# A state-space layer and a mixture of experts on one core: the state's output matmuls contract over 64 rows, in pairs

## What is computed

```
xz = layernorm(x) @ w_in                  # 256 -> 2 * 512, halves xp and z
xc = silu(causal 4-tap conv(xp) + conv_b) # per channel
h[t] = 0.9 * h[t-1] + 0.1 * (xc[t] @ w_B) # the state: 16 numbers per token
y = (h @ w_C) * silu(z)                   # 16 -> 512, gated
x = x + y @ w_out                         # 512 -> 256
n = layernorm(x)
e1, e2 = top 2 of 8 experts by (n[:, 0] @ Wr + br)        # per sequence
x = x + mean over e1, e2 of gelu(n @ W1[e] + b1[e]) @ W2[e] + b2[e]
```

## Time and profile before

| | |
|---|---|
| median of 3 runs | 507.81 us |
| the profiled execution | 506.41 us, of it span 504.6 us |
| PE | busy 499.1 us (99%), 3026 matmuls, granted clock full throughout |
| DVE / ACT / POOL | busy 451.8 (90%) / 400.6 (79%) / 348.7 us (69%) |
| state_out (L1490) | 64 matmuls of 128x512, mean 0.39 us each, 0.23 us from start to start |
| weight loads | 0.19 us each, normally beside the matmul before |

### The profile page before, as it was taken

The page is one execution under the profiler, slowest core; times in us unless marked ns, Lnnn a source line. Parts: engine busy times, 40 slices in busy tenths (PEclk is TensorE's granted clock), DMA queues, the critical chain, the costliest instruction groups (busy, mean ns, idle before and its releaser), DMA issues.

```text
span 504.6 us, 9913 instructions
## 1 busy us (share of the span) xinstructions
PE 499.1 (99%) x3026; PEld 438.7 (87%) x3026; DVE 451.8 (90%) x896; ACT 400.6 (79%) x692; POOL 348.7 (69%) x390
## 2 busy tenths in 40 slices
PE   7999999999999999999999999999999999999997
PEld 7888799888888888888888888888888888888997
DVE  6999899889998899989999899998999989996773
ACT  4986958878869789697887969879797888969454
POOL 4959587659593796928969197782977649773391
PEclk9999999999999999999999999999999999999999
DMA  8940105435251442606235170432604334130102
GB/s 258 292 185 7 37 1 168 125 127 168 73 183 40 162 129 83 208 15 196 81 125 166 42 224 25 166 125 86 205 36 138 117 125 126 52 116 1 42 2 84
DMA packets 53379, 57.28 MB, mean 114 GB/s; under 512 B 8682, under 2 KB 49642, under 8 KB 53226
## 3 DMA queue, kind: packets, MB, share of 16 engines
q1 hardware_dynamic: 51498, 56.67, 34.3%
q10 hardware_dynamic: 1856, 0.31, 0.3%
HBM read 35.46 MB, written 21.50 MB: 113 GB/s over the span
## 4 chain that ended last, share of the span: by engine, by line
PE 97%; DVE 1%; DMA 1%; issue 0%; DVEq 0%
PE blk L1294 16%; PE blk L1295 16%; PE blk L1301 16%; PE tok L1415 12%; PE tok L1417 11%; PE tok L1416 11%; PE turn L1466 3%; PE turn L1469 3%; PE blk L1490 3%; PE turn L1242 1%; PE tok L1294 1%; PE tok L1301 1%; PE tok L1295 1%; DMA x_mid<-in_L_attn_x 1%; DVE stats_t L917 0%; DVE normed L934 0%
## 5 line engine op out<-in xcount | busy, mean ns | idle before, releaser
L992 DVE SCALAR_TENSOR_TENSOR conv<-blk,tap_w,conv 128x512 f32<-128x512 f32 x192 | 130.1, 741 | 7.1 <-ACT conv L683 6.0
L488 POOL TENSOR_TENSOR y_lo<-gate,y_hi 128x512 fp32r<-128x512 f32 x57 | 72.2, 1299 | 35.1 <-ACT y_hi L611 35.1
L1294 PE MATMUL blk<-xn_hi,w_in_hi 128*128 128x512 f32 x228 | 89.4, 392 | 0.0
L1295 PE MATMUL blk<-xn_hi,w_in_lo 128*128 128x512 f32 x228 | 89.0, 391 | 0.0
L453 POOL TENSOR_TENSOR xc_lo<-conv,xc_hi 128x512 fp32r<-128x512 f32 x60 | 73.4, 1242 | 7.5 <-ACT xc_hi L611 7.3
L1415 PE MATMUL tok<-w_out_hi,y_hi 128*128 128x256 f32 x256 | 72.2, 282 | 0.0
L1417 PE MATMUL tok<-w_out_hi,y_lo 128*128 128x256 f32 x256 | 70.8, 277 | 0.0
L1416 PE MATMUL tok<-w_out_lo,y_hi 128*128 128x256 f32 x256 | 70.8, 276 | 0.0
L1301 PE MATMUL blk<-xn_lo,w_in_hi 128*128 128x512 f32 x228 | 70.3, 389 | 0.0
L1415 PE MATMUL tok<-w_hi,hid_hi 128*128 128x256 f32 x248 | 70.3, 283 | 0.0
L683 ACT ACTIVATE conv<-blk,tap_b,tap_w 128x512 f32<-128x512 f32 x64 | 49.1, 778 | 25.1 <-PE blk L1301 22.0
(11 more groups left out here) (189 smaller groups left out, 1318.2 us busy)
## 6 DMA issues: line engine op xcount, KB each, us to landing
spill<-normed SPq DMA_DIRECT2D x25, 512.0 KB, 2.8
normed<-spill SPq DMA_DIRECT2D x100, 128.0 KB, 2.8
out<-x_mid SPq DMA_DIRECT2D x30, 256.0 KB, 2.2
x_mid<-in_L_attn_x SPq DMA_DIRECT2D x29, 256.0 KB, 2.7
x_in<-in_L_attn_x SPq DMA_DIRECT2D x14, 512.0 KB, 4.4
w_all<-in_L_ffn_W SPq DMA_DIRECT2D x2, 2048.0 KB, 11.3
b_all<-in_L_ffn_b SPq DMA_DIRECT2D x1, 1024.0 KB, 13.4
gate<-in_L_attn_w_in SPq DMA_DIRECT2D x2, 256.0 KB, 4.8
```

The lines of the kernel that those rows point to most:

```text
L488: nc.gpsimd.tensor_tensor(y_lo[:, j, :], gate_of(o, j), y_hi[:, j, :].bitcast(F32), ALU.subtract).then_inc(y_lo_set, 1)
L992: nc.vector.scalar_tensor_tensor(cols, blk[j][:], tap_w[:, j, t:t + 1], cols, ALU.mult, ALU.add).then_inc(tap_added, 1)
L1294: mm(dst, whi(k), his(k), start=(k == 0), stop=False)
L1295: ins = mm(dst, wlo(k), his(k), start=False, stop=False)
```

## The change

Weights and state get another layout on the 128 rows: each half of 64 rows (rows 0 to 63, rows 64 to 127) now holds all the products, in four groups of 16, so that 64 rows are enough for one output block. Even blocks j contract over the lower half, odd blocks over the upper.

```
-                    mm(c_bank(a, j)[:], c_mix[:, j * P:(j + 1) * P], state_mix[:], start=True,
+                together = 2 if has_ffn(s) else 1
+                for i, j in enumerate(js):
+                    if i % together == 0:
+                        c_free(a, s, js[i + together - 1])
+                    rows = slice(j % 2 * HALF, (j % 2 + 1) * HALF)
+                    mm(c_bank(a, j)[:], c_mix[rows, j * P:(j + 1) * P], state_mix[rows, :], start=True,
```

```
# ACT state_hi
-                hi(state_mix[:], state[:, q, :]).then_inc(h_hi, 1)
+                hi(state_mix[:], state[:, q, :], sign_rows[STATE][:]).then_inc(h_hi, 1)
# DVE state_lo
-                lo(state_mix[P // 2:P, :], state[P // 2:P, q, :], state_mix[P // 2:P, :]).then_inc(h_lo, 1)
+                nc.vector.scalar_tensor_tensor(state_mix[:], state[:, q, :], low_rows[STATE][:], state_mix[:].bitcast(F32), ALU.mult,
+                                               ALU.add).then_inc(h_lo, 1)
# POOL state_lo, for chunk 1 alone
-                nc.gpsimd.tensor_tensor(state_mix[P // 2:P, :], state[P // 2:P, q, :],
-                                        state_mix[P // 2:P, :].bitcast(F32), ALU.subtract).then_inc(h_lo, 1)
+                nc.gpsimd.tensor_scalar(state[:, q, :], state[:, q, :], low_rows[STATE][:], None, ALU.mult).then_inc(h_masked, 1)
+                pool.wait_ge(h_masked, 1)
+                nc.gpsimd.tensor_tensor(state_mix[:], state[:, q, :], state_mix[:].bitcast(F32), ALU.add).then_inc(h_lo, 1)
# DVE, ahead of everything
+            def row_masks():
+                dve.wait_ge(consts_set, 3)
+                groups = ident[:].rearrange("p (h g i) -> p g h i", h=2, i=NST)
+                for i, group in enumerate(LOW_GROUP):
+                    nc.vector.tensor_reduce(low_rows[i][:], groups[:, group], axis=mybir.AxisListType.XY,
+                                            op=ALU.add).then_inc(rows_set, 1)
+                ...
```

More of the change, by code:

```diff
@@ L36, in build_block @@
     HALO = TAPS - 1
-    REP = P // (2 * NST)
-    assert PER == 2 and TT == 4 and KD == 2 and JD == 4 and JF == 4 and NST == 16 and E == 8
+    HALF = P // 2
+    STATE, WEIGHT = 0, 1
+    LOW_GROUP, REST_GROUP = (1, 2), 3
+    assert PER == 2 and TT == 4 and KD == 2 and JD == 4 and JF == 4 and HALF == 4 * NST and E == 8
     x_t = x.rearrange("b s d -> (b s) d").rearrange("(c n p) d -> c p n d", p=P, n=TT)
@@ L67, in build_block @@
         unused = sb("unused", [1, 1])
+        low_rows, sign_rows = [sb(f"low_rows{i}", [P, 1]) for i in range(2)], [sb(f"sign_rows{i}", [P, 1]) for i in range(2)]
         first_tok = sb("first_tok", [P, KD])
@@ L118, in build_block @@
         consts_set = sem("consts_set")
+        rows_set = sem("rows_set")
         w_hi_set = sem("w_hi_set")
@@ L149, in build_block @@
         u_ready, scanned = sem("u_ready"), sem("scanned")
-        h_hi, h_lo = sem("h_hi"), sem("h_lo")
+        h_hi, h_masked, h_lo = sem("h_hi"), sem("h_masked"), sem("h_lo")
         c_ready = sem("c_ready")
@@ L281, in has_ffn, with mix_cols @@
             return not isinstance(s, int) or s >= 2
+        def mix_cols(h, group):
+            return slice(h * HALF + group * NST, h * HALF + (group + 1) * NST)
         def half_rows(h):
@@ L515, in opening @@
                 norm1(1)
[L516 to L526, removed]
+                pool.wait_ge(w_hi_set, 5 + REST_GROUP)
+                for h in range(2):
+                    nc.gpsimd.tensor_tensor(b_mix[:, :, mix_cols(h, REST_GROUP)], wb_raw[:],
+                                            b_mix[:, :, mix_cols(h, 0)].bitcast(F32), ALU.subtract).then_inc(mix_lo_set, 1)
+                pool.wait_ge(rows_set, 4)
+                nc.gpsimd.tensor_scalar(state[:, 0, :], state[:, 0, :], low_rows[WEIGHT][:], None, ALU.mult).then_inc(mix_lo_set, 1)
+                pool.wait_ge(mix_lo_set, 3)
+                nc.gpsimd.tensor_tensor(c_mix[:], state[:, 0, :], c_mix[:].bitcast(F32), ALU.add).then_inc(mix_lo_set, 1)
+                pool.wait_ge(mix_lo_set, 4)
                 split_conv(0, (0, 1))
@@ L529, in opening @@
                 norm1(2)
-                pool.wait_ge(w_hi_set, 6 + REP)
+                pool.wait_ge(w_hi_set, 6 + REST_GROUP)
                 weights_lo(w_out_lo[:], raw_out, w_out_hi[:])
@@ L627, in mix_hi @@
                 hi(state[:, 0, :], raw_c, GAIN).then_inc(w_hi_set, 1)
[L628 to L631, removed]
+                for group in range(REST_GROUP):
+                    both = b_mix[:].rearrange("p j (h c) -> p j h c", h=2)[:, :, :, mix_cols(0, group)]
+                    hi(both, wb_raw[:].rearrange("p j (o s) -> p j o s", o=1).broadcast_to([P, JD, 2, NST])).then_inc(w_hi_set, 1)
+                act.wait_ge(w_hi_set, 4 + REST_GROUP)
+                act.wait_ge(rows_set, 4)
+                hi(c_mix[:], state[:, 0, :], sign_rows[WEIGHT][:]).then_inc(w_hi_set, 1)
             def turn1_hi(c):
@@ L1074, in route @@
                 nc.vector.max_index(expert[:], best[:], scores[:]).then_inc(route_step, 1)
+            def row_masks():
[4 more added lines that the diff above has]
+                                            op=ALU.add).then_inc(rows_set, 1)
+                for i in range(2):
+                    dve.wait_ge(rows_set, 1 + i)
+                    nc.vector.tensor_scalar(sign_rows[i][:], low_rows[i][:], -2.0, 1.0, ALU.mult, ALU.add).then_inc(rows_set, 1)
             def opening():
+                row_masks()
                 stats1_first(0)
@@ L1102, in opening @@
                 dve.wait_ge(consts_set, 4)
-                dve.wait_ge(mix_lo_set, REP + 2)
+                dve.wait_ge(mix_lo_set, 4)
                 scan(0, 0)
@@ L1472, in state_in, with c_free @@
                 ins.then_inc(u_ready, 1)
+            def c_free(a, s, j):
+                if has_ffn(s):
+                    pe.wait_ge(gelu_set, (s - 2) * JF + j + 1)
+                elif a == 0:
+                    pe.wait_ge(gate_set, JD + j + 1)
+                elif j == 0:
+                    pe.wait_ge(route_step, 1)
+                elif j == 1:
+                    pe.wait_ge(tap_added, last_tap(2, 2))
+                elif j == 2:
+                    pe.wait_ge(gate_set, 3 * JD - 1)
+                else:
+                    pe.wait_ge(tap_added, last_tap(2, 3))
             def state_out(a, s, js=range(JD)):
                 pe.wait_ge(h_lo, a + 1)
[L1476 to L1489, removed]
-                    mm(c_bank(a, j)[:], c_mix[:, j * P:(j + 1) * P], state_mix[:], start=True,
+                together = 2 if has_ffn(s) else 1
[4 more added lines that the diff above has]
+                    mm(c_bank(a, j)[:], c_mix[rows, j * P:(j + 1) * P], state_mix[rows, :], start=True,
                        stop=True).then_inc(c_ready, 1)
@@ L1531, in opening @@
                 pe.wait_ge(gate_set, JD)
-                pe.wait_ge(mix_lo_set, REP + 2)
+                pe.wait_ge(mix_lo_set, 4)
                 state_in(0)
```

## The result

The changed kernel takes 510.5 us (median of 5 runs, 510.14 to 510.66); the kernel before, on the same chip, 507.5 (507.0 to 508.16, 5 runs). The ratio is 1.0057, 95% interval 1.0045 to 1.0068. It is slower by 0.6%, where 506.1 was forecast, and outside the range given (504.3 to 509.8). The profiled execution took 510.5 us with a span of 508.4 us, 3.8 more than before (504.6).

The account below looks back on a forecast made before the run. PE was taken as the bound (97% of the chain of waits), in even steps DVE as much; 3.02 us gained less 1.35 lost made 1.67 better, 506.1 us from a median of 507.81, range 504.3 to 509.8.

Parts of the forecast that it names:

- Changing the shape of the tile: Two tile changes per state_out on PE, taken as costing nothing; upper bound 0.255 us each, 0.51 for both.
- The matmuls: State_out's four matmuls on PE: 0.93 us before, 0.57 forecast, the second of a pair starting 0.11 after the first.
- g: Gain per state_out on PE from running pairs at once: 0.36 us taken, 0.465 if fully abreast.
- rival D: State_out's pairs run fully abreast and POOL's opening mask is short: 504.3 us; chance 0.12.
- the gain of 3.02: Gain in us over steps 2 to 15: 2.16 + 0.29 + 0.32 + 0.25.
- 0.40 in the sum: Loss at xp 0 in even steps 4 to 12, where PE waits for ys: five times 0.08 us.
- the opening: POOL's added mask, 1.1 us, delays w1_lo, so PE loses 0.90 us, bounds 0.3 to 1.65; tile changes 0.05 more.
- B: Rival: each tile change empties the array, 0.51 us per state_out against 0.36 gained; 4.0 slower, 511.8 us; chance 0.10.
- state_hi and state_lo: New per-row forms on ACT (+0.085 us) and DVE (+0.063) make DVE's chain 0.15 later; bounds 0 to 0.3.
- the 0.08 at each even border: Part of DVE's 0.15 us delay that shows at xp 0 in even steps, beyond 0.07 of slack.
- The wait of 0.3 to 0.4 us: Expected sign in the changed profile: PE at xp 0 of even steps waits this long for DVE's gate.
- The borders: Step balance at xp 0: odd steps 3 to 13 gain 0.36 us each, even steps 4 to 12 lose 0.08 each.

Follow-up runs that it names:

- E14: Kernel before, state_out's matmuls over all 128 rows but only 64 of 128 output columns each; 507.11 us, ratio 0.9994.
- E2: Kernel before, all four state_out matmuls cut to rows 0 to 63, so no pairs, products left out; 513.46 us, ratio 1.0123.
- e13: As e11, but in steps 2 to 15 state_out's second pair stands six down matmuls behind the first; 515.46 us, ratio 1.0155.
- e3: Changed kernel with state_out's four matmuls back on 128 rows, masks and layout kept; 508.24 us, ratio 1.0022.
- e1: Kernel before with only state_out's matmuls cut to 64-row pairs, half the products left out, no masks; 509.23 us, ratio 1.0049.
- e11: Kernel before with the 64-row pairs alone, half the products left out, and one needless DVE operation per even step; 507.60 us, ratio 0.9994.
- e5: Changed kernel, POOL copying both W2 halves before subtracting either, without its two waits; 521.64 us, ratio 1.0292.
- e6: Changed kernel with one needless DVE operation ahead of turn2_lo in each even step; 508.63 us, ratio 1.0034.

## Why the prediction was wrong, step by step

- **Changing the shape of the tile**, taken as nothing: this is the step that failed. It is 0.41 us per visit of state_out (0.2 at each change, as two starts that come 0.10 late), between the two ends I had (0 and 0.51). I chose by the nearest row, the scores, and noted myself that those tiles are cut by columns. E14 shows that a change of columns is indeed free and a change of rows is not. The Trainium skill ("TensorEngine Tiling (Array Packing)", Key Properties) says that a change of tiling mode drains the engine. E2 and e13 show a cost of 0.41 us per visit that fits this for rows; by e14 a change from 128 to 64 columns shows nothing of it.
- **The matmuls**, g = 0.36: 0.47 measured, fully abreast (rival D's assumption). The loads of a pair do not go one after the other. The Trainium skill ("TensorE: Matmul & The Clock Gate", Part 3) has the loads of different row groups overlap and the matmuls start some 4 ns apart, and the trace agrees: two matmuls within 0.50 us, their two loads within 0.18. With both terms right, g is 0.47 - 0.41 = 0.06 us, and the gain of 3.02 for the 14 steps is about 0.8.
- **How much each is of the miss.** The span grew by 3.8 us where 1.7 less was forecast, 5.5 apart. The matmuls of steps 2 to 15, both terms together, are 2.2 of it (3.02 against 0.8). The loop's waits are 1.6 (2.0 measured above what the matmuls give, 0.40 in the sum), the opening 1.4, the rest 0.2. With the tile changes alone put right, here and in the opening, the sum would stand near 509, inside my range; the waits in the loop carried it out.
- **Rivals.** B had the mechanism, at 0.25 a change instead of 0.20, but with g at 0.36. Taken with D's g it loses only 0.05 us per state_out, and its opening then makes it 2.5 us slower, 510.3: near the measured 510.5 by luck, since it has nothing for the waits in the loop. I had let each rival change one term. Two ends of my sums are off too: the terms of the unfavourable end give 507.85 and not 507.6, and D's 504.3 is reached, nearly, only without the 0.40 at the even steps.
- **state_hi and state_lo**: 725 ns on ACT (0.72 forecast) and state_lo 0.75 us in odd steps, as forecast. In even steps, beside POOL, state_lo takes 0.92, less than the 1.08 that I had and than the 1.02 of before, and takes back what ACT adds. So the 0.15 is missing there, and the 0.08 at each even border with it: e3 has the masks and no such wait. The wait of 0.3 to 0.4 us that I named as the sign does appear, once at that length and four times at 0.21 to 0.24, but e1 shows it without the masks. The right sign had another cause.
- **The borders.** Missing from the sum is DVE against POOL. I took from the trace that DVE's chain moves with PE's. It meets POOL in the even step, and who goes first costs up to 1.1 us an operation. Between e1 and e11, which differ by the needless operation alone, the 13 steps are 2.3 us apart. That the meeting matters is shown by this; which of its waits makes the first down late was not followed.
- **The opening**: 2.4 us instead of 0.95. POOL's mask took 1.57 us (1.1 taken, bounds 0.56 and 1.83), and PE's waits for w1_lo were 0.67 and 0.49 where I had 0.54 and 0.36; h_lo for chunk 1, called free, made PE wait 0.51. E3 puts the masks' share at 1.2. The tile changes there, 0.05 in the sum, are 0.7 by e1's intervals (21.65 and 19.40 against 21.19 and 19.16). The other 0.5 lie before the first state_out, where e1, the same as before up to that point, also came 0.36 late and e13, the same as e11 up to there, 1.3 later than e11; this I cannot tell from scatter.

## What to carry to other kernels

Matmuls over different halves of the rows do run at once, but PE loses time at both edges of a visit. So count visits, not matmuls: here a pair of 512 columns wins 0.23 us and a visit costs 0.41, so one pair loses 0.18 and two win 0.06. When a profile has to price a new kind of event, ask what differs between it and the nearest row; where the answer is the very thing in question, the row bounds nothing. And before a few tenths on the busiest engine are added up over a loop, look where two other engines hold each other up: one needless operation there moved e1 by half a percent and the changed kernel by a quarter of one.

## What the runs showed of the hardware that was not expected

- A DVE operation of 0.68 us took 4.56 us beside a POOL that went from one operation to the next (e5), and POOL's w_lo, 1.30 us alone, took 2.46 beside DVE (e6).
- Which of the two gets in between two operations of the other is not settled here: in e5 and e6 the one that ran kept going, in the kernel before and in the changed one the other got in.
- An operation on 128x4 numbers took 1.07 to 1.26 us beside a POOL operation, 0.16 alone (changed kernel, e6).
- A POOL multiplication by a value per row over 128x512 took 1.57 us in every kernel that has it, more than POOL's subtraction of two tensors of that size, 1.30.
- Open is why rows cost and columns do not, and what makes the loop settle at 60.6 or 61.1 us for a pair of steps behind different openings.
